# Delta-rule scan of a fused two-layer network: a new order of TensorE's work in each scan step, with ScalarE's order to match

## The reference

```python
def step(carry, xs):
    W_in, W_out = carry
    qi, ki, vi, li, lo, wi, wo = xs
    p_q = softmax(einsum('bnhd,bDhd->bnhD', qi, W_in), axis=1)
    o = einsum('bnhD,bDhd->bnhd', p_q, W_out)
    p = softmax(einsum('bnhd,bDhd->bnhD', ki, W_in), axis=1)
    grad_out = einsum('bnhD,bnhd->bDhd', -p, vi)
    a = einsum('bDhd,bnhd->bnhD', W_out, vi)
    s = sum(p * a, axis=-1, keepdims=True)
    g_z = -(p * a - p * s)
    grad_in = einsum('bnhd,bnhD->bDhd', ki, g_z)
    W_in = wi * W_in - li * grad_in
    W_out = wo * W_out - lo * grad_out
    return (W_in, W_out), o
```

## Time and profile before

| | us |
|---|---|
| three runs | 826.81, 834.0, 831.8; median 831.8 |
| the profiled execution | 833.5 |
| its span, first to last instruction | 831.7 |
| the scan on PE, from the first states_turn to the last | 214.1 to 698.2 |

### The profile page before, as it was taken

The page is one execution under the profiler, slowest core; times in us unless marked ns, Lnnn a source line. Parts: engine busy times, 40 slices in busy tenths (PEclk is TensorE's granted clock), DMA queues, the critical chain, the costliest instruction groups (busy, mean ns, idle before and its releaser), DMA issues.

```text
span 831.7 us, 34224 instructions
## 1 busy us (share of the span) xinstructions
PE 721.9 (87%) x14919; PEld 661.8 (80%) x14920; DVE 626.4 (75%) x1033; ACT 477.4 (57%) x767; POOL 580.4 (70%) x433
## 2 busy tenths in 40 slices
PE   5779737867889999999999999999999999866798
PEld 5366627766789988899988999888988889856698
DVE  6584514547878988899998999999998999684115
ACT  5673113325766775576667668666666766538320
POOL 7530465135889998889988988879787789714640
PEclk9685658989999999999999999999999999967999
DMA  8402313320070000000000000000000000061118
GB/s 327 176 27 77 102 45 77 67 58 17 15 211 10 10 7 6 7 6 7 9 6 7 20 3 3 17 4 3 3 16 4 3 17 17 16 254 26 42 48 292
DMA packets 33583, 42.89 MB, mean 52 GB/s; under 512 B 4000, under 2 KB 25648, under 8 KB 32928
## 3 DMA queue, kind: packets, MB, share of 16 engines
q1 hardware_dynamic: 29856, 33.99, 12.0%
q0 software_dynamic: 3296, 6.76, 3.5%
q10 hardware_dynamic: 288, 0.01, 0.0%
HBM read 26.65 MB, written 14.09 MB: 49 GB/s over the span
## 4 chain that ended last, share of the span: by engine, by line
PE 72%; DVE 9%; issue 7%; another core or an unknown queue 4%; POOL 3%; ACT 2%; DMA 2%; DVEq 1%; ACTq 0%; POOLq 0%; SPq 0%
PE psum L1917 17%; PE psum L1972 7%; PE psum L1950 6%; PE psum L2017 6%; PE psum L1965 4%; PE psum L2008 4%; PE psum L1979 3%; PE psum L1987 3%; PE psum L1855 3%; PE psum L1707 2%; PE psum L1958 2%; PE psum L1865 2%; PE psum L2275 2%; PE psum L2240 1%
## 5 line engine op out<-in xcount | busy, mean ns | idle before, releaser
L1917 PE MATMUL psum<-hT,w_qkv 128*128 128x128 f32 x1408 | 174.0, 280 | 3.9 <-ACT hT L930 1.8
L1917 PEld LDWEIGHTS psum<-hT,w_qkv 128*128 128x128 f32 x1408 | 164.4, 194 | 7.5 <-ACT hT L930 2.0
L619 POOL TENSOR_TENSOR arena<-arena,small 128x1024 f32<-128x1024 f32 x56 | 106.0, 1914 | 41.4 <-DVE small L1461 41.2
L598 POOL TENSOR_TENSOR arena<-arena 128x1024 f32<-128x1024 f32 x56 | 106.6, 1903 | 9.9 <-ACT arena L973 9.4
L584 POOL TENSOR_TENSOR arena<-arena 128x1024 f32<-128x1024 f32 x56 | 106.5, 1902 | 0.1
L1454 DVE TENSOR_REDUCE small<-arena 128x16 f32<-128x1024 f32 x60 | 73.0, 1218 | 10.7 <-ACT arena L962 9.0
L623 POOL TENSOR_TENSOR arena<-arena 128x1024 f32<-128x1024 f32 x28 | 65.8, 2352 | 12.8 <-DVE arena L1481 12.8
L560 POOL DMA_INDIRECT arena<-h_rows,route x39 | 39.6, 1015 | 49.0 <-issue 48.7
L1442 DVE TENSOR_REDUCE small<-psum 128x16 f32<-128x1024 f32 x60 | 72.8, 1215 | 1.0 <-remote 1.0
L1448 DVE TENSOR_TENSOR arena<-psum,small 128x1024 f32<-128x1024 f32 x60 | 70.5, 1215 | 0.1
L2017 PE MATMUL psum<-arena 64*64 64x128 f32 x1792 | 61.9, 276 | 7.1 <-issue 4.5
(11 more groups left out here) (333 smaller groups left out, 1645.4 us busy)
## 6 DMA issues: line engine op xcount, KB each, us to landing
y_rows<-hT SPq DMA_DIRECT2D x8, 512.0 KB
arena<-in_L_W_rows SPq DMA_DIRECT2D x2, 2048.0 KB, 10.7
arena<-y_rows SPq DMA_DIRECT2D x8, 512.0 KB, 7.6
o_rows<-arena SPq DMA_DIRECT2D x9, 256.0 KB
x_sb<-in_x_rows SPq DMA_DIRECT2D x4, 512.0 KB, 6.8
arena<-in_L_W_rows SPq DMA_DIRECT2D x2, 1024.0 KB, 9.7
arena<-in_W_in_rows SPq DMA_DIRECT2D x4, 512.0 KB
arena<-in_W_out_rows SPq DMA_DIRECT2D x4, 512.0 KB
```

The lines of the kernel that those rows point to most:

```text
L598: pool.tensor_tensor(x3, x3, lr[:, tile_of(t) * 32 + k * H:tile_of(t) * 32 + k * H + H].unsqueeze(2).to_broadcast([P, H, D]), ALU.mult).th ...
L619: pool.tensor_tensor(z4, z4, r3.unsqueeze(3).to_broadcast([P, 8, 2, CH]), ALU.mult).then_inc(done, 1)
L1917: mm = pe.matmul(ps[bank][:, p * P:(p + 1) * P], w_qkv[:, j * HD + p * P:j * HD + (p + 1) * P], hT[:, at:at + P], start=True, stop=True)
```

## The change

Four edits, all in the scan. In TensorE's step the key projection is cut in two halves of four matmuls (eight records) each, with `states_q` between them; `states_turn`, with its wait for ktok_out, moves behind the second half; `a_of` moves ahead of `p_turn` and of its wait for silu_k. The wait for win_new now stands ahead of the second half of the key projection and of `states_turn`, since `states_q` carries it; the wait for the freed w_out (wout_new) moves with `states_q`. On ScalarE `oT_of` moves ahead of `k_tanh`, so the order is `k_tok_out`, `exponentials`, `oT_of`, `k_tanh`, `w_outT_out`, `p_tok_out`, `v_tok_out`. On GpSimd `decay_out`, which overwrites w_out, waits for `pe_wt` instead of `pe_ow`, because `states_turn` is now the last of the two reads. No instruction that computes is added or removed.

```diff
--- before.py
+++ after.py
@@ -584,7 +584,7 @@
                 pool.tensor_tensor(w4, w4, d4.unsqueeze(3).to_broadcast([P, 2, HP, D]), ALU.mult).then_inc(done, 1)
 
             def decay_out(t):
-                pool.wait_ge(pe_ow, t + 1)
+                pool.wait_ge(pe_wt, t + 1)
                 after(pool, wout_new, t - 3)
                 decay(w_out, 1, t, wout_dec)
 
@@ -1013,6 +1013,8 @@
                 if 0 <= i - 1 < TU:
                     k_tok_out(i - 1)
                 exponentials(i, 1)
+                if 0 <= i - 1 < TU:
+                    oT_of(i - 1)
                 if 1 <= i and i + 1 < TZ:
                     k_tanh(i + 1)
                 if i == 0:
@@ -1020,8 +1022,6 @@
                     act.activation(junk, ln_eps, ACT.Tanh)
                 if 0 <= i - 1 < TU:
                     w_outT_out(i - 1)
-                if 0 <= i - 1 < TU:
-                    oT_of(i - 1)
                 if 0 <= i - 1 < TU:
                     p_tok_out(i - 1)
                 if 0 <= i - 1 < TU:
@@ -1918,6 +1918,13 @@
                                    start=True, stop=True)
                 mm.then_inc(done, 1)
 
+            def project_half(t, j, bank, k):
+                at = tile_of(t) * P
+                for p in range(k * HP // 2, (k + 1) * HP // 2):
+                    mm = pe.matmul(ps[bank][:, p * P:(p + 1) * P], w_qkv[:, j * HD + p * P:j * HD + (p + 1) * P], hT[:, at:at + P],
+                                   start=True, stop=True)
+                return mm
+
             def half(q):
                 return slice(q * D, q * D + D)
 
@@ -2113,23 +2120,22 @@
                 pe.wait_ge(z_centered, 2 * i - 1)
                 k_turn(i - 2)
                 pe.wait_ge(z_centered, 2 * i)
-                if i < TU:
-                    project(i, 1, 3, pe_pk)
-                else:
-                    project(2 * i - TU + 1, 0, 3, pe_pk)
-                pe.wait_ge(ktok_out, i - 1)
-                after(pe, wout_new, i - 5)
-                states_turn(i - 2)
+                key = (i, 1) if i < TU else (2 * i - TU + 1, 0)
+                project_half(*key, 3, 0)
                 pe.wait_ge(pq_norm, i - 1)
                 after(pe, vT_out, 1 if i == 2 else 0)
+                after(pe, wout_new, i - 5)
                 after(pe, win_new, i - 2)
                 states_q(i - 2)
+                project_half(*key, 3, 1).then_inc(pe_pk, 1)
+                pe.wait_ge(ktok_out, i - 1)
+                states_turn(i - 2)
                 if i >= 3:
                     pe.wait_ge(silu_q, i + 1)
                     grad_out(i - 3)
+                a_of(i - 2)
                 pe.wait_ge(silu_k, i + 1)
                 p_turn(i - 2)
-                a_of(i - 2)
                 if i == 2:
                     pe.wait_ge(silu_q, i + 1)
                 after(pe, wout_new, i - 2)
```

## The result

The changed kernel is slower: 857.81 us in the median of four runs (856.26 to 859.44) against 832.4, a ratio of 1.031 (95% interval 1.027 to 1.035), 25.4 us more. The direction was forecast, the size was not: 843 was said, with a range that ended at 856. The profiled execution took 856.26 us with a span of 854.5, 22.8 more than the span before.

What follows compares the result with a forecast made beforehand. PE was taken to set the pace before; afterwards the loop through DVE's update_in: 17.80 + 0.14 + 0.25 = 18.19 us a step against 17.77, 0.42 more, times 25 is 10.5 us, 842.3 beside the median, rounded up to 843; range 826 to 856.

Steps and rivals of the forecast that it cites:

- the wait of a_of: On PE, a_of behind states_turn waits for w_outT_out on ACT: a new 0.47 us in every step.
- the loop of 17.80 us in point 4: From states_q's start S, weigh at S + 6.99, DVE's return path 10.76, hand-over 0.05: 17.80 us, above PE's 17.11 + 0.47.
- the rates: A group's rates stand in DVE's way between the maxima: 0.14 us a step on top of the loop.
- My 0.25: PE's "issue" pauses between instruction packets, from states_q's start to p_turn: 0.25 us a step, bounds 0 and 0.8.
- About the same: Rival, chance 0.2: the loop closes but costs nothing, with 0.3 us less on the return path or pauses hidden; 832 to 836.
- PE stays the bound: Rival, chance 0.18: old pauses hide in the w_outT wait, step 17.58, 823 us; needs weigh within 6.7 us of states_q's start.
- Much slower: Rival, chance 0.12: 0.8 us of pauses a step move into the loop at grad_out and a_of, ahead of p_turn; 856 us.
- Points 1, 2 and 5: Parts of the forecast: states_q earlier on PE, k_tanh later on ACT, decay_out waiting for pe_wt on POOL; last two cost 0.
- The slack of 0.10 at the read: At states_q on PE: starting 1.64 us earlier leaves 0.10 of the 1.74 us of slack behind update_in.
- The 1.1 us by which k_tanh moves back: On ACT, with k_silu on DVE following: cost 0, covered by DVE's 1.34 us idle; uncovered, at most 1.1 a step less slack.
- decay_out's new wait: On POOL, decay_out waits for pe_wt behind two normalisations that start later: cost 0, at most 1.6 us.
- The 0.41 a step of the old pauses: PE's "issue" pauses before the change on a_of, the turns and grad_out: 11.5 us in all, 0.41 a step.

Runs made afterwards that it cites:

- swap_back: Changed kernel with p_turn and its wait for silu_k ahead of a_of again; 852.80 us, ratio 1.026 to the kernel before.
- spread: Changed kernel with key halves around states_turn, then states_q; a_of before p_turn; w_outT_out and oT_of ahead of k_tanh; ratio 1.032 to the kernel before.

## Why the prediction was wrong in size

The mechanism held, its sizes did not. The bound moved from PE's work to the loop from states_q over w_outT, a_of, p_turn, p_tok_out, weigh and update_in back to states_q; the wait of a_of is 0.43 for 0.47.

**The step that failed is the loop of 17.80 us in point 4; it measured 18.18.** Piece by piece, from the regular step above: k_tanh's start 2.29 for 2.13, a_of 4.28 for 4.13, from there to p_tok_out's start 1.85 for 1.79, to weigh 1.11 for 1.07, weigh to the end of update_in 10.81 for 10.76, and from there to states_q 0.14 for 0.05. No piece is missing. The largest error is half the keys: 0.99, "half of 1.98", measured 1.09 to the next group. The working also took PE's groups by the chain's pieces, which count a group to the start of the next; where another engine takes over, the last group counts to its end, 0.07 later, and this happens twice in the loop, behind the key half and behind p_turn. Together this is 0.24. And I gave all hand-overs 0.05, where those into weigh and into states_q have 0.09 and 0.14; the return path on DVE has 0.05 more. Small terms, but the excess over the step before was itself a small difference: 17.80 + 0.39 - 17.77 = 0.42. An error of 0.38 in it nearly doubles it.

**The balance.** The 25 steps behind the first two take 18.60 us on average: 18.18, 0.11 for the rates (0.46 in six steps), 0.25 for the slow reads, and 0.05 for all other pauses. Forecast was 17.80 + 0.14 + 0.25 = 18.19. So of the 12.4 us that the scan grew beyond my 10.5, 0.38 x 25 = 9.5 are the loop, some 0.6 the other terms, and 2.2 the first two steps, which grew from 39.4 to 41.6 us although I had left them alone. That the other terms come out so near is luck. My 0.25 was for pauses between packets, and those took 0.05; the slow reads, which I did not know, filled it up. In the changed kernel run again they are missing: the 25 steps take 18.42 there, and the scan 502.0 us.

**The rivals.** "About the same" needed 0.3 us less on the return path; it was 0.14 more. "PE stays the bound" needed weigh at S + 6.7 or less, and it was 7.24; with update_in out of the loop the step was not PE's alone either, but that of the way over difference. "Much slower" gave 856 and came nearest in time, but for a reason that is not the main one: it put 0.8 of pauses into the loop, and there were 0.3, most of them not of the kind that it named. My range ended at its price with no room for a loop and pauses that are both longer.

**Points 1, 2 and 5.** The slack of 0.10 at the read never came into play, since the later weigh uses it up in every step. The 1.1 us by which k_tanh moves back were said to cost nothing. In the changed kernel that is nearly so: v_turn waits for update_out 5 times, 2.5 us. swap_back and spread show the price once another order leans on it. decay_out's new wait shows nowhere. The 0.41 a step of the old pauses is 11.5 us over 28 steps; over the 27 of the other terms it is 0.43, which changes nothing.

## What to carry to other kernels

In a pipeline written by hand, list what each consumer needs before moving a producer: here weigh needed two results, which had come side by side, and the new order put them one behind the other. A stage that gives its input's slack away must be paid by the loop that it closes, so sum each loop from a start to the same start, with a group counted to its end wherever another engine takes over, a hand-over for each change of engine, and a group that is cut in two priced above its halves. Then look for the next longest loop, for it limits what opening the first can gain. When such a sum lies within a few per cent of the present step, its error is as large as the answer, and the range must be set by that error.

## What was not expected of the hardware

- Hand-overs differ, even between the same two engines. In the step shown: PE's modelled end to ACT 0.05 (662.09 to 662.14), ACT to PE 0.05 (665.15 to 665.20). ACT to DVE is 0.09 at weigh (668.07 to 668.16) and 0.04 at k_silu. DVE to PE is 0.14 from update_in to states_q (678.97 to 679.11), 0.15 in other steps, and 0.05 from difference to the projection. What makes the difference is not shown. The Trainium skill lists in "Perfetto Trace Analysis", in its summary of the profiler window per engine type, what the shown window of VectorE and ScalarE leaves out, the decoding and the way of the semaphore among it, and for TensorE that the end is estimated; the trace here shows such gaps and does not divide them.
- Eight matmul records of the 128-row kind take 1.09 us to the next group, sixteen 1.98.
- An engine can have more idle time and be in the loop that sets the pace all the same: DVE is busy for 622.8 us after and 626.4 before, and one reduction of 1.22 us costs 1.15 a step after and 0.14 before.
- The kernel before took 831 to 832 us on some occasions and 801 to 804 on others, also on the same chip. The changed kernel's two profiles, spans of 854.5 and 818.3, show where: 20 us ahead of the scan, 4.5 in it and 11 behind it. Ahead of the scan the granted clock was 0.81 in the first (0 to 211.3 us) and 0.85 in the second (0 to 190), behind it 0.86 and 0.91. What set it is open.
